# Masks copied by DMA, and offsets made in three row tiles instead of four

## What is computed

```python
xdw = depthwise_3x3(x) + dw_b
om = (xdw @ om_w + om_b).reshape(n, h, w, G, 27)     # G = 8 groups
offset, mask = om[..., :18].reshape(..., 9, 2), om[..., 18:]
py, px = base_y + ky + offset[..., 1], base_x + kx + offset[..., 0]
# sampled: bilinear sample of value at (py, px), zero outside the image
out = einsum('nhwgkc,nhwgk->nhwgc', sampled, mask) @ op_w
```

## Time and profile before

| | |
|---|---|
| median of 3 runs | 456.26 us (456.15 to 458.84) |
| profiled execution, its span (the page gives no other time for it) | 457.2 us |
| until the first product on DVE | 30.1 us |
| images 0 to 6, to the first product of image 7 | 200 us |
| image 7 and the end of the convolution | 27 us |
| token stage | 200 us |
| busy in the whole span: PE, DVE, ACT, POOL | 410.0, 335.2, 259.5, 141.3 us |

### The profile page before, as it was taken

How to read it: one execution, slowest core, us unless ns; L and a number is a source line. 1 busy time by engine, 2 the same in 40 slices (tenths; PEclk the granted TensorE clock), 3 DMA queues, 4 the chain that set the end, 5 groups by cost and what they waited for, 6 DMA issues and landing times. The chain is left out here.

```text
span 457.2 us, 9731 instructions
## 1 busy us (share of the span) xinstructions
PE 410.0 (90%) x3276; PEld 232.0 (51%) x3276; DVE 335.2 (73%) x730; ACT 259.5 (57%) x571; POOL 141.3 (31%) x172
## 2 busy tenths in 40 slices
PE   1689999999999999999998457989999999999995
PEld 0543343433534335343332345867677776767663
DVE  3479967789777897777889346768777686868652
ACT  2683645746457464574610154676767677685752
POOL 2263223243232422324200164123242333324322
PEclk9979999999999999999999655799999999999997
DMA  8068886938559385583860330000000000000000
GB/s 258 3 155 218 215 222 148 229 89 227 163 122 231 91 226 158 117 239 86 226 162 1 141 134 0 2 0 2 2 0 14 3 0 14 1 2 1 11 3 11
DMA packets 28409, 44.91 MB, mean 98 GB/s; under 512 B 6864, under 2 KB 11088, under 8 KB 27984
## 3 DMA queue, kind: packets, MB, share of 16 engines
q1 hardware_dynamic: 28368, 44.39, 37.6%
HBM read 6.11 MB, written 0.52 MB: 15 GB/s over the span
## 5 line engine op out<-in xcount | busy, mean ns | idle before, releaser
L663 DVE TENSOR_TENSOR prod<-ps_t,a_rep 128x1024 f32<-128x1024 f32 x128 | 152.0, 1219 | 34.5 <-PE ps_t L363 32.3
L363 PE MATMUL ps_t<-b,vt 32*128 32x512 f32 x512 | 74.7, 650 | 1.9 <-DVE prod L663 1.9
L769 POOL TENSOR_TENSOR a<-a,mask 128x512 f32<-128x512 f32 (+1 forms) x40 | 47.0, 1178 | 83.7 <-ACT a L523 81.4
L383 PE MATMUL ps_d<-prod,keep 128*32 128x512 f32 x512 | 69.0, 611 | 0.3 <-DVE prod L663 0.2
L1223 POOL TENSOR_TENSOR total<-total,share 128x256 f32<-128x256 f32 x56 | 40.9, 730 | 86.9 <-DVE share L1117 86.5
L304 PEld LDWEIGHTS ps_m<-om_r,sel 128*128 128x128 f32 x193 | 29.0, 187 | 75.3 <-ACT mask L501 28.2
L1101 DVE TENSOR_TENSOR hidden<-ps_h,gated 128x256 f32<-128x256 f32 x128 | 51.4, 415 | 3.7 <-ACT gated L1316 2.8
L1316 ACT ACTIVATE gated<-ps_h 128x256 f32<-128x256 f32 x128 | 47.8, 387 | 7.5 <-PE ps_h L1436 1.1
L304 PE MATMUL ps_m<-om_r,sel 128*128 128x256 f32 x193 | 49.3, 334 | 0.0
L1117 DVE TENSOR_TENSOR share<-ps_yf,factor 128x256 f32<-128x256 f32 x56 | 23.7, 423 | 30.4 <-issue 12.8
L1310 ACT ACTIVATE factor<-ps_yf 128x256 f32<-128x256 f32 x64 | 24.6, 385 | 37.3 <-PE ps_yf L1471 37.3
(11 more groups left out here) (151 smaller groups left out, 671.3 us busy)
## 6 DMA issues: line engine op xcount, KB each, us to landing
a_rep<-a SPq DMA_DIRECT2D x128, 256.0 KB, 4.7
a_rep<-a SPq DMA_DIRECT2D x32, 128.0 KB, 2.8
w_f<-in_w SPq DMA_DIRECT2D x2, 1024.0 KB, 5.8
start<-in_start SPq DMA_DIRECT2D x1, 1344.0 KB, 7.8
x_turned<-in_x_turned SPq DMA_DIRECT2D x1, 512.0 KB, 3.8
t_tok<-in_x SPq DMA_DIRECT2D x1, 512.0 KB, 9.4
w<-in_w SPq DMA_DIRECT2D x1, 512.0 KB, 7.6
select_f<-in_select SPq DMA_DIRECT2D x1, 512.0 KB, 8.4
```

The costliest lines, as they stand in the source:

```text
L363: mm = pe.matmul(out, vt[par][r, v % 2, :, :, :].rearrange("p j y c -> p (j y c)"), b[par][r, pair_taps(v // 2), :].rearrange("p t x -> p ...
L383: mm = pe.matmul(ps_d[r, :], fold[:, v % 2, :], p, start=v == 0, stop=False, skip_group_check=True)
L663: dve.tensor_tensor(p[:, :, :], t[:, :, :], a_rep[par][:, ms, pair_taps(v // 2), :].rearrange("p m t x -> p m (t x)"), ALU.mult).then_inc( ...
L769: pool.tensor_tensor(v, v, mask[(PAIRS * par + k) % 2][:, 0:wide, :], ALU.mult).then_inc(a_done, 1)
```

## The change

The five mask jobs go. Their place is taken by nine DMAs an image on SP's queue: each reads 8 partitions of `om_f` (one tap's masks, 1 KB each) sixteen times and writes the 128 partitions of that tap in `mask`, which is now one tile for all nine taps. The masks are needed in `om_f` alone, so a tile of 128 rows now holds Y and X of three taps twice (the value and its rounding error) and three sets of mask rows once, and three tiles hold all: the second half of the offsets is one tile. PE's job slots 5, 7, 10, 12 and 14 are free, and the nine jobs left keep about the places that they had. SP issues the masks of image n after the fills of image n - 1 and before those of image n. ACT's copy of the offsets waits for the last image's mask DMAs, whose source it overwrites, and for the last image's masking.

```diff
-QUADS = 4
+QUADS = 3
-SELS = 9
+SELS = 6
-        mask = [sb(f"mask{i}", [P, 2, PIX]) for i in range(2)]
+        mask = sb("mask", [P, TAPS, PIX])
+        mask_in = [sem(f"mask_in{k}") for k in range(PAIRS)]
-        REPS = [(Y, 0), (M, 0), (Y, 1), (M, 1), (X, 0), (Y, 2), (M, 2), (Y, 3), (M, 3), (Y, 4), (M, 4),
-                (X, 1), (X, 2), (X, 3)]
+        REPS = [(Y, 0), (Y, 1), (X, 0), (Y, 2), (Y, 3), (Y, 4), (X, 1), (X, 2), (X, 3)]
+        REP_AT = {4: 0, 6: 1, 8: 2, 9: 3, 11: 4, 13: 5, 15: 6, 16: 7, 17: 8}
+        def mask_rows(k):
+            return [(tap, tap // 3, (48, 56, 112)[tap % 3]) for tap in range(2 * k, min(2 * k + 2, TAPS))]
+        def masks_in(k, images):
+            return 16 * len(mask_rows(k)) * images
+            def masks(n):
+                halves = [count(sp, 2 * n + half + 1) for half in range(2)]
+                for k in range(PAIRS):
+                    if k in (0, 3):
+                        sp.wait_ge(om_copied, halves[k // 3])
+                    for tap, q, row in mask_rows(k):
+                        src = om_f[row:row + GROUPS, q, :]
+                        sp.dma_start(mask[:, tap, :], src.unsqueeze(1).broadcast_to([GROUPS, P // GROUPS, PIX]))\
+                          .then_inc(mask_in[k], 16)
+            masks(0)
             fill(0, 0)
+            masks(1)
             fill(1, 1)
...
+                    masks(2 * it + par)
                     fill(2 * it + par, par)
...
-                for q in range(2):
+                for q in range(2 - half):
                     mm = pe.matmul(bank[:, q * PIX:(q + 1) * PIX], om_w[h:h + 64, 2 * half + q, :],
...
@@ copy_offsets
+                if positive(n):
+                    for k in (range(3) if half == 0 else range(3, PAIRS)):
+                        act.wait_ge(mask_in[k], masks_in(k, n))
+                    if half == 0:
+                        act.wait_ge(a_done, PAIRS * n)
...
@@ copy_rep
-                if kind == M:
-                    if positive(PAIRS * n + k - 1):
-                        act.wait_ge(a_done, PAIRS * n + k - 1)
-                    wide = 2 if k < PAIRS - 1 else 1
-                    act.activation(mask[(PAIRS * par + k) % 2][:, 0:wide, :].rearrange("p t x -> p (t x)"),
-                                   ps_m[:, 0:wide * PIX], ACT.Copy).then_inc(rep_out, 1)
-                    return
...
@@ masked
                 pool.wait_ge(a_hat, PAIRS * n + k + 1)
-                if isinstance(n, int) and n == 0:
-                    pool.wait_ge(first_out, BY_DVE.index((M, k)) + 1)
+                pool.wait_ge(mask_in[k], masks_in(k, n + 1))
                 v = a[:, pair_taps(k), :]
-                wide = 2 if k < PAIRS - 1 else 1
-                pool.tensor_tensor(v, v, mask[(PAIRS * par + k) % 2][:, 0:wide, :], ALU.mult).then_inc(a_done, 1)
+                pool.tensor_tensor(v, v, mask[:, pair_taps(k), :], ALU.mult).then_inc(a_done, 1)
...
```

More of the change, by code:

```diff
@@ L297, in spread_out @@
             def spread_out(kind, k, bank):
[L299 to L304, removed]
+                parts = [(2 * k, kind), (2 * k + 1, kind)] if k < PAIRS - 1 else [(TAPS - 1, Y), (TAPS - 1, X)]
+                for s, (tap, axis) in enumerate(parts):
+                    mm = pe.matmul(bank[:, s * PIX:(s + 1) * PIX], sel[:, tap % 3 + 3 * axis, :], om_r[:, tap // 3, :],
                                    start=True, stop=True)
@@ L401, in ahead_of @@
                 kind, r = JOBS[s - 1]
+                if kind == "free":
+                    return ahead_of(s - 1, n, slab, par, out)
                 if kind == "out":
@@ L554, in reps @@
             def reps(n, npar, slab):
-                for r, (kind, k) in enumerate(REPS):
+                behind = 0
+                for s, r in REP_AT.items():
                     copy_rep(r, n, npar)
-                    if r and REPS[r - 1][0] != M:
-                        hat(r - 1, n, npar)
+                    while behind < (r if s + 1 in REP_AT else r + 1):
+                        hat(behind, n, npar)
+                        behind += 1
                     if r == XV_AT and slab is not None:
                         values_in(slab)
-                hat(len(REPS) - 1, n, npar)
+                hat(len(REPS) - 1, n, npar) if behind < len(REPS) else None
             def image(i, par, slab, made):
@@ L1534, in shape_arrays @@
         for part in (0, 64):
[L1535 to L1536 removed]
+            sel[part + 8 * which + at // 16, which, at] = 1.0
+        if which < 3:
             sel[ROWS, which], sel[ROWS + 1, which] = -(at % 16), 1.0
[L1538 removed]
+        else:
             sel[ROWS, which], sel[ROWS + 2, which] = -(at % 16), 1.0
@@ L1545, in shape_arrays @@
     for q in range(QUADS):
[L1546 to L1549, removed]
+        for row, tap, kind in places(q):
+            kernel_at[row:row + 8, q] = (tap % 3 - 1, tap // 3 - 1, 0)[kind]
     select = np.zeros((P, EXPERTS // 2, 2, C), np.float32)
@@ L1563, in places @@
     y, x, m = 1, 0, 2
-    rows = [(2 * q, y), (2 * q + 1, y), (2 * q, x), (2 * q + 1, x), (2 * q, m), (2 * q + 1, m)]
-    return rows + ([(TAPS - 1, (y, x, m)[q])] if q < 3 else [])
+    spots = [(part + 8 * (3 * at + r), 3 * q + r, kind) for part in (0, 64) for at, kind in enumerate((y, x))
+             for r in range(3)]
+    return spots + [(row, 3 * q + r, m) for r, row in enumerate((48, 56, 112))]
 def laid_out(inputs, np):
```

45 lines of the change are left out of this document (17 added, 28 removed).

## The result

The changed kernel takes 501.31 us (median of 4 runs, 497.56 to 503.01) against 457.30 us before (4 runs, 456.15 to 458.84): a ratio of 1.095, 95% interval 1.089 to 1.100. The profiled execution took 497.56 us, the least of the four; its span is 495.8 against 457.2, so the profile shows 38.6 of the 44.0 us between the medians.

The account below looks back on a forecast made before the run. PE bounds the kernel before at 28.56 us an image; after, masks plus fills on the DMA engines. Start +10, seven images +67 and last image 0 give +77 on 456.3: 533 us, range 474 to 595.

Parts of the forecast that it names:

- What bounds the image: On SP's queue masks and fills take turns: 17 + 21.1 = 38.1 us an image against 28.56 before.
- F: Time of one image's fills on the DMA engines: 4.72 MB at 224 GB/s, 21.1 us.
- M: Time the DMA engines take for an image's nine mask copies, 1.18 MB: taken at 17 us.
- The two nearer readings: For the mask copies: a quarter of the settled 224 GB/s, 21 us; three masks under way at 91 GB/s, 13 us.
- Rival C: Only half the engines carry a mask, its source having 8 partitions: M 10.6, image 31.7, 482 us; chance 0.15.
- Start: Image 0: DVE's second product waits for masks and the first pair's fills, +9 us and 1 for slow beginning: +10.
- Seven images: Seven images at 38.1 us instead of 28.56: +67 us.
- cover: Waits of POOL's masking and ACT's offsets copy add nothing, as other masks and fills keep the engines busy meanwhile.
- Last image and clock: Last image: DVE's pace covers its fills, 0; PE's lower clock costed at nothing, except a microsecond or two there.
- What PE saves: Selecting jobs and an offsets matmul go from PE: 2.6 us an image, 18 us over seven images.
- Rival D: Masks move like the fills, in the 7.5 us the engines are free: image 26.4 us, -15, 441 us; chance 0.12.
- the reading that was forecast: Case A: M between 13 and 21, image 34.1 to 42.1 us, 501 to 565 us in all; chance 0.55.

Follow-up runs that it names:

- step4: The changed kernel with each mask DMA reading every fourth partition out of 32 instead of 8 neighbours (values not the masks'): 455.27 us, ratio 0.993.
- src16: The changed kernel with each mask DMA reading 16 neighbouring partitions eight times instead of 8 sixteen times (values not the masks'): 462.64 us, ratio 1.011.
- step16: The changed kernel with all nine mask copies reading rows 0, 16, ... 112, every sixteenth partition (values not the masks'): 495.72 us, ratio 1.080.
- same8: The changed kernel with all nine mask copies reading rows 48 to 55 instead of three groups in turn: 589.67 us, ratio 1.285.
- spread: The changed kernel with each tap's eight mask rows laid on every fourth partition, offsets on the rows between, nothing left out: 454.29 us, ratio 0.9925.
- nomask: The changed kernel with the nine mask copies made for image 0 alone, later images using its masks: 456.60 us, ratio 0.995.
- nomask_taps: nomask with VectorE's nine depthwise product steps cut from 16 rows to one for images 2 to 7: 452.45 us, ratio 0.988.

## Why the prediction was right

Right in sign and mechanism; one term was taken half as large again as it was, for a wrong reason, and one was worth less than it was counted.

- **What bounds the image.** Predicted: masks and fills in turn, 38.1 us. Measured: the same turn, 33.1 us. The runs show it by dose: masks of 5.9, 7.0, 9.7, 11.3 and 18.6 us of the queue (step4, src16, step16, the change, same8) give 455, 463, 496, 501 and 590 us.
- **F.** 21.1 us predicted, 20.6 to 21.9 measured over the eight images.
- **M, the term that was mis-sized.** Taken at 17 us; measured are 11.3 us of issue and 11.5 to 12.0 for the copies themselves. The two nearer readings were 13 and 21, the bounds 5.3 and 39. The step that failed is "the number of source partitions being read sets the rate". With 8 rows read it was 52, 100, 103 or 195 GB/s, by which rows. The first microsecond of the first fill, on which the readings were scaled, was no price for it. The estimate by the ports of the Trainium skill (SBUF — State Buffer, Door 1: The DMA port swizzle), 21.7 us for one copy at a time, is met by same8 (128 KB at 52 GB/s, nine times: 22.7 us); the change, with its three groups in turn, moved twice as fast.
- **Rival C** had an M near the measured one, 10.6 (482 us), and its share of about a half is there. Its reason is not: step4 moves twice as much at that share.
- **Start.** +10 predicted, +5.2 measured (first product at 35.31 instead of 30.13). Putting 12.0 in for 17 in the prediction's own sum makes it 5.0.
- **Seven images.** +67 predicted, 231.7 - 199.9 = +31.8 measured. With M at 12.0 the working gives 33.1 us an image and +31.8, so turn and cover were right. (11.3, the issue alone, gives 32.4 and +27.)
- **Last image and clock.** 0 predicted, with a microsecond or two named for the clock and left out of the sum; its stretch is 1.4 us longer. Its first products wait for a DMA, and the granted clock is 0.90 over it against 0.95.
- **What PE saves.** 18 us, which "no longer matter" in the forecast: true there. Rival D had made 441 us of it with masks at the fills' rate. step4 and spread come close to that condition (M 5.9 for 5.3) and end at 455 and 454, some 13 us above it. By D's own working M of 5.9 gives 27.0 us an image and 445; measured are 27.9, the queue's turn with its pauses. And without any masks behind image 0's (nomask) the images still keep only 6.8 of the 18 us, as those with depthwise steps gain nothing.
- **Token stage.** Unchanged, 200.1 against 199.8 us.
- **The total.** M of 12 lies just outside the reading that was forecast (13 to 21). With it the sum is 493 us. The last image and the token stage add 1.7 us, the fourth run of the kernel before 1.0 to its median, and the medians lie 5.4 us further apart than the two profiled executions, which no profile explains. That these bring the time to 501, the lower end of the forecast reading, is luck.

## What to carry to other kernels

Before moving a job from an engine onto DMAs, ask of the copies which partitions they read, not only how many bytes: eight rows read sixteen times moved at 52 to 195 GB/s according to where they lay, and laying them on every fourth partition cost no measurable time here. Add copies that stand in one queue to the transfers already there, and compare the sum with the time that the engines leave free. And an engine that has no idle time can hide the waits of its partner: here, taking work from it paid in the images where the partner had time left, and not in the others.

## What the runs showed of the hardware

- Copies from 16 neighbours moved 150 GB/s at a DMA share of 0.80; copies from 8 spaced rows moved 195 at 0.56. A busy share alone does not tell the rate.
- Slow copies cost the engine that issues them: the same mask issue took SyncE 0.61 us in step4, 1.25 in the change and 2.53 in same8 (medians). Six held ScalarE 7.4 to 12.8 us with neighbouring rows and 3.8 to 10.3 with spaced ones. On SyncE nine never took under 5.8 us.
- A VectorE step on 16 columns took 226 ns, one on 256 columns 475 ns (medians in nomask_taps and nomask): a sixteenth of the work, about half the time. Some steps of either kind took far longer, up to 1.1 and 1.25 us.
